# A linear-attention and convolution kernel: image stores in halves, with one semaphore per half, in place of quarters

## What is computed

```python
x = x + _L0_conv_ref(_gn(x), g, w_qkv, mem_kv, w_out, b_out)   # linear attention, 4 heads of 32
x = x + _L1_conv_ref(_gn(x), w3, w1, b, 4)                     # 3x3 convolution
```

## Time and profile before

| | us |
|---|---|
| median of 3 runs | 1963.32 |
| lowest and highest | 1957.2, 1964.3 |
| the profiled execution | 1962.26 |
| its span | 1960.5 |

### The profile page before, as it was taken

How to read it: one execution, slowest core, us unless ns; L and a number is a source line. 1 busy time by engine, 2 the same in 40 slices (tenths; PEclk the granted TensorE clock), 3 DMA queues, 4 the chain that set the end, 5 groups by cost and what they waited for, 6 DMA issues and landing times.

```text
span 1960.5 us, 51383 instructions
## 1 busy us (share of the span) xinstructions
PE 1861.5 (95%) x21521; PEld 993.2 (51%) x21521; DVE 1632.6 (83%) x3108; ACT 1369.6 (70%) x1480; POOL 1311.3 (67%) x729
## 2 busy tenths in 40 slices
PE   3799999999999999999999999999999999999997
PEld 1455554555554555544555544555544555544552
DVE  6778888888888788888888888888888888888874
ACT  4677776776776777766777766777676777766761
POOL 6476767686666676767676767676667686667670
PEclk8989999999999999999999999999999999999999
DMA  6267877887877797877788878787877797877765
GB/s 130 46 139 157 178 165 155 169 176 160 171 164 161 150 180 157 178 164 159 162 181 152 178 162 157 163 181 150 180 160 161 157 182 156 177 165 157 156 145 145
DMA packets 349430, 313.01 MB, mean 160 GB/s; under 512 B 299152, under 2 KB 299920, under 8 KB 341008
## 3 DMA queue, kind: packets, MB, share of 16 engines
q1 hardware_dynamic: 346656, 305.75, 75.3%
q10 hardware_dynamic: 2224, 3.97, 0.8%
q0 software_dynamic: 320, 0.01, 0.0%
HBM read 68.10 MB, written 67.11 MB: 69 GB/s over the span
## 4 chain that ended last, share of the span: by engine, by line
PE 54%; SPq 21%; DVE 18%; DMA 4%; issue 2%; ACT 1%; POOL 0%; ACTq 0%; DVEq 0%; POOLq 0%
PE pair_ps L922 18%; PE pair_ps L904 8%; DVE km L1286 7%; SPq L334 6%; SPq L321 5%; PE pair_ps L913 5%; PE pair_ps L863 4%; SPq L333 4%; DVE u L1283 4%; DVE image L1338 4%; PE pair_ps L885 3%; PE bank_ps L814 3%; DMA replicas<-yg_lo 3%; PE pair_ps L823 3%; SPq L306 2%; SPq L327 2%
## 5 line engine op out<-in xcount | busy, mean ns | idle before, releaser
L922 PE MATMUL pair_ps<-replicas,w_rep 96*32 96x512 f16 x8192 | 490.3, 383 | 18.0 <-DMA replicas<-yg_lo 18.0
L489 POOL TENSOR_TENSOR u_lo<-u,u_hi 128x1024 f16<-128x1024 f32 x128 | 269.9, 2139 | 280.2 <-ACT u_hi L608 280.2
L492 POOL TENSOR_TENSOR exp_kT_lo<-exp_kT,exp_kT_hi 128x1024 f16<-128x1024 f32 x128 | 273.1, 2134 | 192.8 <-ACT exp_kT_hi L620 190.2
L922 PEld LDWEIGHTS pair_ps<-replicas,w_rep 96*32 96x32 f16 x8192 | 201.6, 96 | 279.8 <-issue 76.7
L495 POOL TENSOR_TENSOR u_lo<-exp_q,u_hi 128x1024 f16<-128x1024 f32 x128 | 270.4, 2142 | 25.7 <-ACT u_hi L626 25.2
L608 ACT ACTIVATE u_hi<-u 128x1024 f16<-128x1024 f32 x128 | 135.3, 1057 | 144.5 <-DVE u L1283 137.5
L1338 DVE SCALAR_TENSOR_TENSOR image<-pair_ps,image 128x512 f32<-128x512 f32 x256 | 175.5, 686 | 45.3 <-PE pair_ps L922 41.3
L626 ACT ACTIVATE u_hi<-exp_q 128x1024 f16<-128x1024 f32 x128 | 131.5, 1050 | 109.2 <-DVE exp_q L1325 109.0
L485 POOL TENSOR_SCALAR u<-image,st 128x1024 f32<-128x1024 f32 x128 | 179.3, 1409 | 29.4 <-DVE st L1222 29.4
L863 PE MATMUL pair_ps<-wqk_hi,u_hi 128*128 128x128 f16 x1024 | 181.5, 222 | 0.0
L1325 DVE TENSOR_TENSOR exp_q<-exp_q,pair_ps 128x1024 f32<-128x1024 f32 x128 | 152.9, 1216 | 32.8 <-PE pair_ps L823 29.8
(11 more groups left out here) (184 smaller groups left out, 4500.2 us busy)
## 6 DMA issues: line engine op xcount, KB each, us to landing
image<-in_x SPq DMA_DIRECT2D x256, 256.0 KB, 4.8
out<-image SPq DMA_DIRECT2D x502, 128.0 KB, 2.3
replicas<-yg_hi SPq DMA_DIRECT2D x252, 165.0 KB, 3.7
replicas<-yg_hi SPq DMA_DIRECT2D x252, 107.2 KB, 2.4
replicas<-yg_lo SPq DMA_DIRECT2D x126, 165.0 KB, 4.2
replicas<-yg_lo SPq DMA_DIRECT2D x126, 107.2 KB, 2.3
uT_hi<-u_hi SPq DMA_TRANSPOSE x128, 4.4
uT_lo<-u_lo SPq DMA_TRANSPOSE x128, 4.0
```

Source lines behind the costliest of these rows:

```text
L489: pool.tensor_tensor(px(UL, v), px(U, v), px(UH, v), ALU.subtract).then_inc(ul_ready, 1)
L492: pool.tensor_tensor(KL[:, v % 2], KT[:, v % 2], KH[:, v % 2], ALU.subtract).then_inc(kl_ready, 1)
L922: mm = pe.matmul(conv_ps[32 * r:32 * r + 32, j % 2], w_rep[0:32 * SLOTS, tap, r], rep[:, j * ROWS + dy:(j + 1) * ROWS + dy, dx:dx + SIDE], ...
```

## The change

Stores are made of half an image with 256 KB in each of the four DMAs, and the four semaphores become two. `store(s, h)` takes a half. In a step, `store(e, 2)` behind chunk 5 is gone, and `store(e, 1)` behind chunk 7 stores both quarters 2 and 3; `store(c, 0)` stands behind chunk 3 and stores quarters 0 and 1, and nothing is stored behind chunk 1. The load of a half waits for the semaphore of that half. The drain keeps its stores of quarters (`store_part`), which now raise the semaphore of their half, and the counts at the end of the program follow from that. In the programs of TensorE and DVE a few pairs of waits that stand ahead of the same instruction are written in the other order.

```diff
-        stored = [sem(f"stored{u}") for u in range(UNITS)]
+        stored = [sem(f"stored{h}") for h in range(2)]
...
-            def store(s, v):
-
+            def store(s, h):
+
+                cols = slice(h * PIX // 2, (h + 1) * PIX // 2)
                 for r in range(RES):
-                    sp.dma_start(out_dram[s, r][:, v * UNIT:(v + 1) * UNIT],
-                                 px(image(s), v)[32 * r:32 * r + 32]).then_inc(stored[v], 16)
+                    sp.dma_start(out_dram[s, r][:, cols], image(s)[32 * r:32 * r + 32, cols]).then_inc(stored[h], 16)
...
             def step(p, a, c, e):
                 if p is not None and p >= PRELOADED:
                     if e is not None:
                         sp.wait_ge(stored[0], at(e, 16 * RES, 16 * RES))
                     if e is not None:
-                        sp.wait_ge(stored[1], at(e, 16 * RES, 16 * RES))
+                        sp.wait_ge(stored[0], at(e, 16 * RES, 16 * RES))
                     load(p, 0)
-                if e is not None:
-                    sp.wait_ge(out_ready, at(e, CHUNKS, 6))
-                    store(e, 2)
                 if a is not None:
                     sp.wait_ge(ul_ready, at(a, UNITS, 1))
                     turn_u(a, 0)
                 if e is not None:
                     sp.wait_ge(out_ready, at(e, CHUNKS, 8))
-                    store(e, 3)
+                    store(e, 1)
...
                     if e is not None:
-                        sp.wait_ge(stored[3], at(e, 16 * RES, 16 * RES))
+                        sp.wait_ge(stored[1], at(e, 16 * RES, 16 * RES))
                     if e is not None:
-                        sp.wait_ge(stored[2], at(e, 16 * RES, 16 * RES))
+                        sp.wait_ge(stored[1], at(e, 16 * RES, 16 * RES))
                     load(p, 1)
...
-                    sp.wait_ge(out_ready, at(c, CHUNKS, 2))
+                    sp.wait_ge(out_ready, at(c, CHUNKS, 4))
                     store(c, 0)
-                    sp.wait_ge(out_ready, at(c, CHUNKS, 4))
-                    store(c, 1)
...
-            for v in range(UNITS):
-                sp.wait_ge(stored[v], 16 * RES * batch)
+            for h in range(2):
+                sp.wait_ge(stored[h], 16 * RES * (batch + 1 + h))
...
+                    pe.wait_ge(k_max, at(a, 8, 8))
                     pe.wait_ge(ul_ready, at(a, UNITS, 1))
-                    pe.wait_ge(k_max, at(a, 8, 8))
                     keys(a, 0, pair_ps[2])
```

More of the change, by code:

```diff
@@ L364, in store_part @@
                     sp.dma_start(out_dram[s, r][:, v * UNIT:(v + 1) * UNIT],
-                                 px(image(s), v)[32 * r:32 * r + 32]).then_inc(stored[v], 16)
+                                 px(image(s), v)[32 * r:32 * r + 32]).then_inc(stored[v // 2], 16)
             def step(p, a, c, e):
@@ L1005, in step @@
                     keys(a, 3, pair_ps[0])
+                    pe.wait_ge(kl_ready, at(a, UNITS, 1))
                     pe.wait_ge(uT_in[0], at(a, 32, 32))
-                    pe.wait_ge(kl_ready, at(a, UNITS, 1))
                     context(a, 0, bank_ps[0])
@@ L1036, in step @@
                     denominators(a, 3, bank_ps[1])
+                    pe.wait_ge(uT_in[3], at(a, 32, 32))
                     pe.wait_ge(kl_ready, at(a, UNITS, 4))
-                    pe.wait_ge(uT_in[3], at(a, 32, 32))
                     context(a, 3, bank_ps[0])
@@ L1096, in step @@
                 if c is not None:
+                    pe.wait_ge(hi_in[1], at(c, 16 * 2 * RES, 16 * 2 * RES))
                     pe.wait_ge(lo_in[1], at(c, 16 * RES, 16 * RES))
-                    pe.wait_ge(hi_in[1], at(c, 16 * 2 * RES, 16 * 2 * RES))
                     conv_ring(c, 3)
@@ L1404, in step @@
                 if c is not None:
+                    dve.wait_ge(hi_ready, at(c, UNITS, 1))
                     dve.wait_ge(yg_ready, at(c, UNITS, 1))
-                    dve.wait_ge(hi_ready, at(c, UNITS, 1))
                     low_y(c, 0)
@@ L1419, in step @@
                 if c is not None:
+                    dve.wait_ge(yg_ready, at(c, UNITS, 3))
                     dve.wait_ge(hi_ready, at(c, UNITS, 3))
-                    dve.wait_ge(yg_ready, at(c, UNITS, 3))
                     low_y(c, 2)
```

## The result

The changed kernel takes 2083.10 us (median of 4 runs, 2067.17 to 2087.34), the kernel before 1963.81 us beside it. The ratio is 1.0603, with a 95% interval of 1.0577 to 1.0629. The prediction said 1995 us in a range of 1968 to 2012 us: the sign was right, the size was not, and the measured time lies far outside.

The account below looks back on a forecast made before the run. Two nearly equal paths bound each step: TensorE's own work and SP's DMA list up to L922. Nine steps plus nineteen steps of later release gave 28 to 37 us; the middle, 33, on 1962.26 gave 1995 us, range 1968 to 2012.

Parts of the forecast that it names:

- The ring: TensorE's matmuls at L922, which need SP's low replicas; they start at +25.13 us with no DMA wait, else at +25.46.
- moment zero: SP's issue of the store behind chunk 7, from which each step is measured; 28 periods of 58.80 us on average.
- The end of the step costs nothing: Behind chunk 3, the doubled store delays load(p, 0) from 919.40 to about 921.7; covered, with about 0.4 us to spare.
- The new wait is covered by turn 1: Before load(p, 1), the wait for the stored half is mostly covered: store landed by about +6.0, turn 1's transfers until +8.0.
- The shift of SP's release: SP is released from turn 2's low half at +13.5 instead of +12.49 or +11.79: 1.0 or 1.7 us later.
- The other value: Second estimate of SP's later release: 2.3 us in steps without a DMA wait at L922, 1.2 us in the others.
- the late kind: Nineteen of 28 periods, where L922 waits for the replicas; the step shown starts it at +25.46, period 58.45 us.
- 0.7 us of slack in nine steps: In the nine steps where L922 starts at +25.13, the last replica was taken to land 0.7 us ahead of it.
- The holds of about 1 us: Something held SP about 1.0 us in the first six us of some steps; behind a longer store this would be hidden.
- rival 3: Faster: SP's holds fall outside zero to +25 in its shorter stream, transfer hidden too; -19 us, 1943 us; chance 0.04.
- far slower: Wait for the stored half not covered by turn 1; each step pays 2.3 and 0.4 us; 70 us, 2032 us; chance 0.06.
- (1): No visible change: writes run beside the transposes, added half moves in half the time; 6 us, 1968 us; chance 0.13.

Follow-up runs that it names:

- first half alone: Changed kernel with the second half stored again in two quarters behind chunks 5 and 7, first half still one store behind chunk 3: 1970.37 us, ratio 1.0054.
- filler of 12: Changed kernel plus 12 matmuls whose results nobody uses, ahead of TensorE's wait for the replicas: 2041.66 us, ratio 1.0422.
- half a megabyte that nobody waits for: Kernel before plus four DMAs of 128 KB from a constant tile, right behind the store of quarter 3: 2083.16 us, ratio 1.0619.

## Why the prediction was right or wrong

- **What bounds the kernel, and where.** Right. The ring waits for the end of SP's list, the extra half megabyte at moment zero is nearly the whole matter, and removing it removes the loss but for 0.3%.
- **The end of the step costs nothing.** Nearly right: 0.5% with the first half alone, of which 0.1% is a later ring. The wait for stored[0] is 3.4 us on average (99.0 us in 29 times), as forecast (near 4 us), and is covered.
- **The new wait is covered by turn 1.** Right as far as it goes: the wait for the stored half does not show at all. But the reason was not the one given. SP itself is late by then.
- **The shift of SP's release, +13.5 against +12.49 and +11.79.** This step failed. The term is the later ring, put at 33 us (1.2 us a step); it measured 62 us (2.2 us a step). The end of a chain of transfers was set against releases read from the trace. The same chain for the kernel before, with half a megabyte of stores, gives 0.8 + 2.3 + 2.6 + 4.8 + 0.7 = +11.2, which is 0.6 and 1.3 us earlier than the releases that were read, and this error of the chain was taken off the shift. Like against like it is 2.3 us in either kind of step. The other value took 1.1 us off in the late kind, because a hold would be hidden behind a longer store; no row showed that. With 2.3 us everywhere, and the 0.7 us of slack in nine steps, the sum would have been 28 x 2.3 - 9 x 0.7 = 58 us. The timelines show where the shift stands:

| mean of 28 steps, us, from SP's store | before | changed |
|---|---|---|
| four stores, time to issue | 1.73 | 2.86 |
| turn 1, high half | 1.56 | 2.68 |
| turn 1, low half | 1.44 | 1.51 |
| load(p, 1) begins | 4.93 | 7.25 |
| from there to SP's release | 7.35 | 7.40 |
| SP's release | 12.29 | 14.65 |
| from there to the low replicas | 8.94 | 8.78 |

  The whole shift, 2.36 us, is there before the load begins, and nothing behind it takes it up. The prediction counted four stores at 0.43 us each, and looked for the hold in the low half of turn 1; it stands in the stores and in the high half. The size of one store isn't what holds SP: in the changed kernel the four issues take 0.33, 0.42, 0.59 and 1.23 us (medians of 61 stores), before 0.32, 0.42, 0.43 and 0.42. The first two are alike; only with the first stores ahead of them are the third and fourth held. Eight issues of 128 KB are not held, but it comes to the same: stores and turn 1 together take 7.0 us with eight issues and 7.1 us with four, on average. The windows of one step of the changed kernel (zero at 924.76) show the DMA engines busy without a break; the middle one, in which turn 1's transposes run, has a DMA share of 1.15 but moves 133 GB/s, where the sum had taken 212 GB/s for turn 1.

```profile
925.60:930.20 4.60, 4.60 (x68) 3.80 (x66) 3.75 (x9) 4.16 (x6) 0.70 (x1) 1.00 0.98 222
930.20:934.40 4.20, 4.20 (x73) 3.87 (x71) 3.81 (x14) 3.81 (x5) 4.12 (x3) 1.00 1.15 133
934.40:939.20 4.80, 4.74 (x60) 3.53 (x58) 4.08 (x6) 3.72 (x4) 4.80 (x4) 1.00 1.03 221
```

- **The holds of about 1 us.** The prediction ties them to the place in SP's own stream (rival 3) and lets a longer store hide one. The traces tie them to something else. The one in the late kind (the load issued from 935.54 to 938.33) has a 16 KB packet of the queue of instructions at 935.62, and so have 50 of the 55 plain issues of SP in the kernel before that took over 0.5 us longer than is usual for their line (a packet from 0.5 us ahead to the issue's end). The number of these packets is the same with 1782 DMAs issued by SP (before) and with 1538 (changed), and larger in the changed kernel with the filler of 12, which has 372 matmuls more (queue and kind; packets, MB, share; the second line is the filler's):

```profile
q8 instruction: 171, 2.80, 0.6%
```
```profile
q8 instruction: 174, 2.85, 0.6%
```

  So their number follows TensorE's program, and a shorter list of SP doesn't take them away. That the packets cause the holds is not shown.
- **The clock.** This term was missing altogether, the second failure. I had read the granted clock of 0.989 as a constant, and did not ask what a wait of 2 to 3 us before a burst of matmuls would do to it. The rival "far slower" priced only the longer wait. The trace of the kernel before held the effect once: of its 28 periods one is 61.85 us, with the ring at +27.20 and 34.65 us behind it instead of 32.99, and the rule "the period grows by the wait, us for us" doesn't hold for it. The runs without filler show its size: with 25.8 to 25.9 us to the ring one, two or four steps of 28 are low, with 27.1 us twelve, with 28.0 us between 17 and 23; at most 36.2 - 33.0 = 3.2 us each. The Trainium skill, page "TensorE: Matmul & The Clock Gate", section "Part 1: The HAM clock gate", states that the array falls to half rate when it has been idle and comes back when it is busy. The trace agrees: 3.22 us idle, and a granted clock of 0.50 for the ring behind it. A prediction that names a longer wait of TensorE must price the matmuls behind it at either clock. This term measured 55 us.
- **DVE's reading of the load is covered.** Right in effect: DVE now waits 41.9 us for loads (5.9 us before in the same list), and waits 41.8 us for TensorE's group means at L1201 where it waited 78.1 us before; the one took the place of the other.
- **Bounds.** The range's upper end was set at 1.8 us a step. The delay alone, 2.2 us, lies beyond it. It was built from two readings of one term, both of which took something off the 2.3 us of the transfer, and so it did not hold the error that they shared.
- **The rivals.** (3), faster by holds that fall elsewhere, and (1), writes that run beside transposes, did not happen; the run with half a megabyte that nobody waits for excludes (1) directly. (2) named 2.5 us a step, near the 2.2 us of the later ring, but by luck: its cause, a wait for the stored half, does not show.

What stays open: why steps with equal waits fall now in the one, now in the other class of the clock; what holds SP's third and fourth issue and turn 1, beyond that it goes with the bytes ahead of them; and what the run with the first half alone loses outside its 28 steps.

## What to carry to other kernels

When one engine's list of DMA issues ends just ahead of what the busiest engine needs, count bytes that stand ahead in the queue as well as issues, and apply every hold seen once to each place where the same pair (a large transfer, then a transpose) will stand. Merging stores saves issues only where issuing was late; if it moves bytes from a slack stretch to a tight one, it costs their transfer time in each step. Compare a modelled time with the model of the kernel before, and not with its trace, or the model's error goes into the difference. Any new wait of TensorE should be priced twice, once for itself and once for the matmuls behind it at the lower clock; if that matters, a few matmuls of filler bought back 1.8 points of 6.0 here, and two issues moved to another queue 4.9.

## What the runs showed of the hardware

- Four stores of 256 KB (rows of 8 KB) held SP for 2.69 to 2.71 us in most cases, four of 192 KB for 2.2 to 2.4 us, four of 128 KB for 1.71 to 1.73 us; four loads of 256 KB held it for 1.7 to 1.9 us. The time over 1.7 us stands in the third and fourth issue (0.59 and 1.23 us), the first two take what those of 128 KB take.
- The low half of a transposition takes SP 1.31 to 1.33 us when it isn't held, and behind a load up to 4.8 us in the kernel before and 4.7 us in the changed one; the high half takes 1.23 to 1.31 us when it isn't held, and behind a megabyte of stores took 2.7 us on average (1.75 to 2.95).
- Added, useless matmuls made a kernel 1.7% faster (ratios 1.0603 and 1.0422), as they kept TensorE's clock: no low step, against 23.
- SP's holds of about 1 us stand, 50 of 55 times, at a 16 KB packet of the queue of instructions, whose number goes with TensorE's matmuls (171, and 174 with 372 more) and not with SP's DMAs.
